# One array tile shape of 64 rows by 64 columns for all stages of a filtered leaky ReLU

## The reference

```python
x = x + sin(W @ coord + b[:, None, None])           # (512, 256, 256), the same for both images
out = x + bias[None, :, None, None]
out = sep_upfirdn(out, up_filter * 2, up=2)          # 256 -> 512 along each axis, 12 taps
out = leaky_relu(out, 0.2) * sqrt(2)                 # on 512 x 512
out = sep_upfirdn(out, down_filter, down=2)          # 512 -> 256 along each axis, 12 taps
```

## Time and profile before

| | |
|---|---|
| runs | 6846.39, 6847.44, 6847.50 us; median 6847.44 us |
| profiled execution | 6846.66 us, its span 6844.9 us |
| TensorE matmul (PE) | 6782.4 us, 99% of the span, 148480 records |
| TensorE weight load (PEld) | 6303.4 us, 92% |
| VectorE (DVE) | 3954.3 us, 58% |
| ScalarE (ACT) | 4084.0 us, 60% |
| GpSimd (POOL) | 1296.0 us, 19% |
| DMA | 82 GB/s over the span |

### The profile page before, as it was taken

One profiled execution on the slowest core, in us unless ns is written; L12 is line 12 of the kernel. 1 busy time (PEld: TensorE's weight loads), 2 busy tenths in 40 slices (PEclk: granted clock), 3 DMA queues, 4 the chain that ended last, 5 costly groups with the idle time before them and its releaser, 6 DMA issues.

```text
span 6844.9 us, 361569 instructions
## 1 busy us (share of the span) xinstructions
PE 6782.4 (99%) x148480; PEld 6303.4 (92%) x148480; DVE 3954.3 (58%) x6218; ACT 4084.0 (60%) x7688; POOL 1296.0 (19%) x1041
## 2 busy tenths in 40 slices
PE   6999999999999999999999999999999999999999
PEld 6999999999999999999999999999999999999998
DVE  6555555555555555555555555555555555555555
ACT  4566566655666665566566656656665665666555
POOL 2111111111111111111111111111111111111111
PEclk9999999999999999999999999999999999999999
DMA  3222222222222222222222222222222222222222
GB/s 116 81 81 81 80 81 81 81 81 81 80 80 81 81 80 81 81 81 81 80 81 81 81 81 81 80 80 81 81 80 81 81 81 80 80 81 81 81 81 74
DMA packets 580065, 558.27 MB, mean 82 GB/s; under 512 B 40400, under 2 KB 574928, under 8 KB 580048
## 3 DMA queue, kind: packets, MB, share of 16 engines
q1 hardware_dynamic: 580048, 558.02, 25.8%
HBM read 278.94 MB, written 278.92 MB: 82 GB/s over the span
## 4 chain that ended last, share of the span: by engine, by line
PE 99%; DVE 1%; issue 0%; DMA 0%; ACT 0%; SPq 0%; DVEq 0%
PE y_ps L450 34%; PE p_ps L434 34%; PE o_ps L434 15%; PE a_ps L450 14%; PE o_ps L460 3%; DVE up_band L377 0%; DVE angle L354 0%; DVE angle L352 0%; DVE phase L344 0%; ACT trig L258 0%; DVE trig_parts L361 0%; DVE angle L356 0%; DVE turns L348 0%; DVE turns L350 0%; DVE trig_parts L360 0%
## 5 line engine op out<-in xcount | busy, mean ns | idle before, releaser
L392 DVE SCALAR_TENSOR_TENSOR z<-y_ps,leak 128x512 f32<-128x512 f32 x4096 | 2716.1, 684 | 1522.9 <-ACT leak L278 1522.9
L278 ACT ACTIVATE leak<-y_ps 128x512 f32<-128x512 f32 x4096 | 2245.3, 605 | 1024.0 <-PE y_ps L450 1024.0
L450 PE MATMUL y_ps<-up_band,a_sb 64*128 64x138 f32 (+2 forms) x32768 | 2807.5, 288 | 1.6 <-ACT a_sb L271 1.5
L434 PE MATMUL p_ps<-down_band,z 128*64 128x68 f32 (+1 forms) x65536 | 2445.9, 227 | 1.8 <-DVE z L392 1.0
L434 PEld LDWEIGHTS p_ps<-down_band,z 128*64 128x64 f32 x65536 | 2156.2, 137 | 267.3 <-DVE z L392 1.3
L450 PEld LDWEIGHTS y_ps<-up_band,a_sb 64*128 64x128 f32 x32768 | 2228.7, 186 | 148.7 <-issue 1.8
L245 POOL TENSOR_TENSOR x_sum<-x_raw,f_sb 128x512 f32<-128x512 f32 x1024 | 1283.6, 1281 | 5514.0 <-ACT f_sb L264 5504.6
L400 DVE COPY p_rows<-p_ps 128x512 f32<-128x512 f32 x2048 | 1411.0, 689 | 1350.4 <-PE p_ps L434 1277.0
L271 ACT COPY a_sb<-a_ps 128x512 f32<-128x512 f32 x2048 | 1100.3, 589 | 1179.8 <-PE a_ps L450 1179.8
L450 PE MATMUL a_ps<-up_band,x_sum 64*128 64x138 f32 (+2 forms) x16384 | 1297.0, 275 | 26.7 <-POOL x_sum L245 26.6
L434 PE MATMUL o_ps<-down_band,p_rows 128*64 128x68 f32 (+1 forms) x32768 | 1171.0, 224 | 0.7 <-issue 0.7
(11 more groups left out here) (28 smaller groups left out, 40.7 us busy)
## 6 DMA issues: line engine op xcount, KB each, us to landing
x_raw<-in_x_dram SPq DMA_DIRECT2D x1024, 256.0 KB, 2.7
out_dram<-o_out SPq DMA_DIRECT2D x1024, 256.0 KB, 2.1
f_rows<-trig_dram SPq DMA_DIRECT2D x512, 20.0 KB
trig_dram<-trig_parts SPq DMA_DIRECT2D x32, 256.0 KB, 2.5
trig_dram<-ones SPq DMA_DIRECT2D x4, 256.0 KB, 2.3
trig_dram<-bias_wide SPq DMA_DIRECT2D x4, 256.0 KB, 2.5
up_taps<-in_L_conv_up_filter_dram SPq DMA_DIRECT2D x1, 6.0 KB, 2.3
down_taps<-_L_conv_down_filter_dram SPq DMA_DIRECT2D x1, 6.0 KB, 2.4
```

The costliest lines, as they stand in the source:

```text
L278: nc.scalar.mul(leak[i % 2][:, :], y_ps[i][:, :], SLOPE * GAIN).then_inc(leak_done, 1)
L392: nc.vector.scalar_tensor_tensor(z[n][:, i, :], y_ps[i][:, :], GAIN, leak[i % 2][:, :], ALU.mult, ALU.max).then_inc(z_done, 1)
L434: last = nc.tensor.matmul(out_ps[half * HALF:(half + 1) * HALF, lo:hi], data[:, t, col:col + HALF], down_band[:, band:band + hi - lo], sta ...
L450: last = nc.tensor.matmul(outs[o][:, lo:hi], data[row, k, (at + o) * P:(at + o + 1) * P], up_band[row, band:band + hi - lo], start=step == ...
```

## The change

All four filter stages and the Fourier term use four tiles of 64 rows by 64 columns. A down stage is now made like an up stage, in two steps with the row tiles changing banks; each 64-row tile covers 36 or 40 output columns. `p_ps` becomes two banks; `o` is written into the banks of `a`, the Fourier term into the two high banks of `y_ps`. The Fourier term is a product of three float32 rows, kept twice (for both row tiles); the split in high and low parts goes. One of the two copies of `a` moves from ScalarE to VectorE (`copy_a1`), behind z1. Every step begins with `pe.sem_inc(steps_begun, 1)`; in the built program that is an event instruction of TensorE's sequencer, and the waits written ahead of it are carried by it or by sequencer instructions in front of it. TensorE's loop body is one channel.

A slot of image m has 13 steps in this order: Y0 step 0, P0 step 0, Y0 step 1, P0 step 1, Fourier (n = 0 only), A step 0, P1 step 0, A step 1, P1 step 1, Y1 step 0, O step 0, Y1 step 1, O step 1. Y0 and Y1 are the bank pairs of `up_cols` of image m, P0 and P1 the two halves of `down_rows` of image m-1 (over z0 and z1, then z2 and z3), A is `up_rows` of image m+1 and O is `down_cols` of image m-2.

Core of the diff (declarations, the setup of the Fourier rows and the unchanged parts of `slot` are cut):

```diff
-    UP_SPAN = [(0, 262, 6), (250, 512, 0)]
+
+    UP_SPAN = [[(0, 132, 6), (122, 260, 128)], [(250, 388, 0), (378, 512, 128)]]
 
-    DN_SPAN = [(0, 68, 4), (60, 132, 0), (124, 196, 0), (188, 256, 0)]
-
-    PE_CHANNELS = 2
-    assert (C - 2) % PE_CHANNELS == 0
+    DN_SPAN = [[(max(0, 32 * g - 4), min(H, 32 * g + 36), max(0, 32 * g - 4) + 4 - 64 * (g // 2)) for g in (2 * k, 2 * k + 1)]
+               for k in range(UT)]
...
-        p_ps = pb("p_ps", [P, 2, H])
-        o_ps = pb("o_ps", [P, HT, WID])
+        p_ps = [pb(f"p_ps{o}", [P, 2, H]) for o in range(2)]
...
+            def copy_a1(m, n):
+
+                dve.wait_ge(a_made, m + 1)
+                reached(dve, y_made, 4 * m - 4)
+                nc.vector.tensor_copy(a_sb[n][:, 1, :], a_ps[1][:, :]).then_inc(a1_copied, 1)
...
+            def copy_p(m, n):
+
+                dve.wait_ge(p_made, m + 1)
+                reached(dve, o_made, m - 1)
+                for o in range(2):
+                    nc.vector.tensor_copy(p_rows[n][:, 2 * o:2 * o + 2, :], p_ps[o][:, :, :]).then_inc(p_copied, 1)
+
+            def slot(c, n, a_next=True, y=True, p=True):
                 m = 2 * c + n
                 if y:
                     leaky(m, n, 0)
+                    leaky(m, n, 1)
+                if a_next:
+                    copy_a1(m + 1, 1 - n)
                 if p:
-                    copy_p(m - 1, 1 - n, 0)
-                if y:
-                    leaky(m, n, 1)
-                if p:
-                    copy_p(m - 1, 1 - n, 1)
+                    copy_p(m - 1, 1 - n)
                 if y:
                     leaky(m, n, 2)
                     leaky(m, n, 3)
...
+            def step_of(outs, data, band, spans, at, where, ks, step, fresh):
+
+                pe.sem_inc(steps_begun, 1)
+                for k in ks:
                     for rows in range(2):
                         o = rows ^ step
                         row = slice(rows * HALF, (rows + 1) * HALF)
-                        lo = max(0, 256 * k + 128 * rows - 6)
-                        hi = min(UP, 256 * k + 128 * rows + 132)
-                        band = lo + 6 - 256 * k
-                        last = nc.tensor.matmul(outs[o][:, lo:hi], data[row, k, (at + o) * P:(at + o + 1) * P],
-                                                up_band[row, band:band + hi - lo], start=step == 0 and k == 0,
-                                                stop=step == 1 and k == HT - 1, skip_group_check=True)
+                        lo, hi, start = spans[k][rows]
+                        for half in range(2):
+                            col = (at + o) * P + half * HALF
+                            last = nc.tensor.matmul(outs[o][half * HALF:(half + 1) * HALF, lo:hi],
+                                                    data[row, where[k], col:col + HALF],
+                                                    band[row, start:start + hi - lo],
+                                                    start=fresh and step == 0 and k == 0,
+                                                    stop=step == 1 and k == len(spans) - 1, skip_group_check=True)
                 return last
 
             def sines(c):
 
-                pe.wait_ge(f_rows_loaded, 16 * c + 16)
-                reached(pe, o_copied, 2 * c - 4)
+                pe.wait_ge(f_rows_loaded, 32 * c + 32)
+                reached(pe, z_done, 8 * c - 8)
+                pe.sem_inc(steps_begun, 1)
                 for t in range(HT):
-                    last = nc.tensor.matmul(o_ps[:, t, :], f_rows[:, t * P:(t + 1) * P], f_rows[:, H:H + WID],
-                                            start=True, stop=True)
+                    row = slice(t * HALF, (t + 1) * HALF)
+                    for half in range(2):
+                        col = t * P + half * HALF
+                        last = nc.tensor.matmul(y_ps[2 + t][half * HALF:(half + 1) * HALF, 0:WID],
+                                                f_rows[row, col:col + HALF], f_rows[row, H:H + WID],
+                                                start=True, stop=True, skip_group_check=True)
                 last.then_inc(f_made, 1)
 
             def up_rows(m, n, step):
                 if step == 0:
                     pe.wait_ge(x_summed, m + 1)
-                    reached(pe, a_copied, m)
-                    up(x_sum[n], a_ps, 0, 0).then_inc(a_half, 1)
+                    reached(pe, o_copied, m - 3)
+                    reached(pe, a0_copied, m)
+                    reached(pe, a1_copied, m)
+                    step_of(a_ps, x_sum[n], up_band, UP_SPAN, 0, range(HT), range(HT), 0, True).then_inc(a_half, 1)
                 else:
                     pe.wait_ge(a_half, m + 1)
-                    up(x_sum[n], a_ps, 0, 1).then_inc(a_made, 1)
-
-            def up_cols(m, n, pair, step):
+                    step_of(a_ps, x_sum[n], up_band, UP_SPAN, 0, range(HT), range(HT), 1, True).then_inc(a_made, 1)
+
+            def up_cols(m, n, pair, step, f_done=0):
                 outs = y_ps[2 * pair:2 * pair + 2]
                 if step == 0:
                     if pair == 0:
-                        pe.wait_ge(a_copied, m + 1)
+                        pe.wait_ge(a0_copied, m + 1)
+                        pe.wait_ge(a1_copied, m + 1)
+                    else:
+                        pe.wait_ge(f_copied, f_done)
                     reached(pe, z_done, 4 * m + 2 * pair - 2)
-                    up(a_sb[n], outs, 2 * pair, 0).then_inc(y_half, 1)
+                    step_of(outs, a_sb[n], up_band, UP_SPAN, 2 * pair, range(HT), range(HT), 0,
+                            True).then_inc(y_half, 1)
                 else:
                     pe.wait_ge(y_half, 2 * m + pair + 1)
-                    up(a_sb[n], outs, 2 * pair, 1).then_inc(y_made, 2)
-
-            def down_rows(m, n, i):
-                if i == 0:
-                    pe.wait_ge(z_done, 4 * m + 4)
-                reached(pe, p_copied, 2 * m + i)
-                for j in range(2):
-                    last = down(z[n], p_ps[:, j, :], (2 * i + j) * P, j == 0)
-                last.then_inc(p_made, 1)
-
-            def down_cols(m, n, f_done):
-                pe.wait_ge(p_copied, 2 * m + 2)
-                reached(pe, o_copied, m)
-                pe.wait_ge(f_copied, f_done)
-                for t in range(HT):
-                    last = down(p_rows[n], o_ps[:, t, :], t * P, t == 0)
-                last.then_inc(o_made, 1)
+                    step_of(outs, a_sb[n], up_band, UP_SPAN, 2 * pair, range(HT), range(HT), 1,
+                            True).then_inc(y_made, 2)
+
+            def down_rows(m, n, late, step):
+
+                if step == 0:
+                    pe.wait_ge(z_done, 4 * m + 2 * late + 2)
+                    if not late:
+                        reached(pe, p_copied, 2 * m)
+                if step or late:
+                    pe.wait_ge(p_part, 3 * m + 2 * late + step)
+                for pair in range(2):
+                    last = step_of([p_ps[o][:, pair, :] for o in range(2)], z[n], down_band, DN_SPAN, 2 * pair,
+                                   range(UT), (2 * late, 2 * late + 1), step, pair == 0)
+                last.then_inc(p_made if late and step else p_part, 1)
+
+            def down_cols(m, n, step):
+                if step == 0:
+                    pe.wait_ge(p_copied, 2 * m + 2)
+                    step_of([a_ps[t][:, 0:WID] for t in range(HT)], p_rows[n], down_band, DN_SPAN, 0,
+                            (0, 2, 1, 3), range(UT), 0, True).then_inc(o_half, 1)
+                else:
+                    pe.wait_ge(o_half, m + 1)
+                    step_of([a_ps[t][:, 0:WID] for t in range(HT)], p_rows[n], down_band, DN_SPAN, 0,
+                            (0, 2, 1, 3), range(UT), 1, True).then_inc(o_made, 1)
 
             def slot(c, n, a_next=True, f_next=True, y=True, p=True, o=True, f_done=None):
                 m = 2 * c + n
                 if y:
                     up_cols(m, n, 0, 0)
+                if p:
+                    down_rows(m - 1, 1 - n, 0, 0)
+                if y:
+                    up_cols(m, n, 0, 1)
+                if p:
+                    down_rows(m - 1, 1 - n, 0, 1)
+                if f_next and n == 0:
+                    sines(c + 1)
                 if a_next:
                     up_rows(m + 1, 1 - n, 0)
-                if y:
-                    up_cols(m, n, 0, 1)
-                if f_next and n == 0:
-                    sines(c + 1)
                 if p:
-                    down_rows(m - 1, 1 - n, 0)
-                if y:
-                    up_cols(m, n, 1, 0)
+                    down_rows(m - 1, 1 - n, 1, 0)
                 if a_next:
                     up_rows(m + 1, 1 - n, 1)
+                if p:
+                    down_rows(m - 1, 1 - n, 1, 1)
+                if y:
+                    up_cols(m, n, 1, 0, c + 2 if f_done is None else f_done)
+                if o:
+
```

(22 more changed lines are left out.)

114 lines of the change are left out of this document (42 added, 72 removed).

## The result

The changed kernel takes 6996.95 us (median of 4 runs, 6993.4 to 7001.07) beside 6846.91 us: a ratio of 1.0219, 95% interval 1.0202 to 1.0237. It is **slower by 150 us**, where 6650 us and "faster" were forecast.

What follows compares the result with a forecast made beforehand. TensorE, busy 99%, was taken as the bound; with the change a channel lasts 12.85 us instead of 13.23, so 6846.7 - 195 (512 channels) - 2 (setup) = 6650 us, range 6430 to 6880 us.

Steps and rivals of the forecast that it cites:

- the new ring through the copy of `a`: O's first step waits for both copies of `a`, whose banks it shares; round trips of 6.04 and 6.81 us.
- the changes of shape: Switching between the up and down filters' array shapes on TensorE costs 0.70 us an image, which would go.
- Rival four: Weights do not bound a TensorE pass, so a down step is 0.29 us: about 6240 us; chance 0.04.
- Rival one: TensorE's run ahead is kept per tile, sixteen instructions for four tiles, hiding more of the gaps: 6510 us; chance 0.22.
- the turn: At TensorE's loop turn, sequencer instructions outlast the queued matmuls and leave a gap of 0.55 us.
- Rival three: Four tiles do not run side by side; loads wait for matmuls on the same rows: about 8650 us; chance 0.06.
- Rival two: Events keep TensorE's weights from being loaded ahead, so the first load behind each lies open: 7100 us; chance 0.10.
- the sum of the ring: Terms from one O step to the next, over both slots, make a channel of 12.85 us.
- The copy's handoff: From the end of `a` on TensorE to the start of VectorE's copy, in slot n = 0: 0.22 us.
- the margin: The forecast saving per channel: 0.38 us, from 13.23 to 12.85 us.
- Slot n = 0: Slot with the loop turn and Fourier; `a` itself, later than z1, decides when its copy starts: 6.81 us.
- Slot n = 1: Slot without Fourier; path runs through ScalarE's leak, z0, z1, then VectorE's copy of `a`: 6.04 us.

Runs made afterwards that it cites:

- 2: Changed kernel with both copies of `a` on ScalarE and none on VectorE: 7366.37 us, ratio 1.076.
- 3: Changed kernel without TensorE's doubled waits, `a` one p step earlier, and VectorE copying `a` ahead of z1: 6486.28 us, ratio 0.9474.
- 4: Changed kernel without TensorE's doubled waits, `a` one p step earlier, VectorE in its old order (z0, z1, `a`): 6587.39 us, ratio 0.9619.
- 6: Changed kernel with 32 instead of 36 to 40 columns in every down filter pass: 6997.8 us, ratio 1.0221.
- 5: Changed kernel with a second sequencer event ahead of every second step, 12 more a channel: 7352.26 us, ratio 1.0741.
- 10: Changed kernel with one channel less written out ahead of TensorE's loop, which starts at channel 2: 7077.47 us, ratio 1.0336.
- 9: Changed kernel with two channels instead of one in TensorE's loop body: 13052.21 us, ratio 1.9068.
- 1: Changed kernel with TensorE's doubled waits dropped (those an earlier wait already covers): 6830.67 us, ratio 0.9976.
- 11: Changed kernel with one channel less written out ahead of TensorE's loop and 32 events (2 KB) put there: 6989.28 us, ratio 1.0209.

## Why the prediction was wrong

**What held.** The mechanism did in the main: the new ring through the copy of `a` paces both slots (2 to 4), the changes of shape cost nothing (the chain), and columns don't pace a down step (6). Rival four falls with the down step itself (0.46 us for its 0.29), and 6 shows that columns don't set it. Rival one falls with the turn, which shows 0.61 us (0.41 and 0.67 - 0.47) and not 0.39. Rival three falls with the down step: eight passes of four tiles in 0.46 us are 0.058 us each, less than a load (0.055 for 64 columns, the prediction's estimate) and its stream (0.034) one after the other. The Trainium skill's rule that weight loads overlap matmuls only in another row group (TensorE: Matmul & The Clock Gate, "Part 3: Packing small matmuls") doesn't hold for these tiles either, and its 60 cycles a matmul (TensorEngine Tiling, "Instruction Overhead") aren't charged to the engine as a whole: 32 matmuls in 0.46 us are 14 ns each. Rival two came to the right side of no change, with 7100 us, yet by luck: no load lies open behind every event, they show where two or more stand together (5).

**The step that failed is the sum of the ring.** The copy's handoff was nearly twice its term (0.39 us for 0.22), nearly all other terms were a little too small, and the margin was 0.38 us of 12.85. By term, measured against forecast (a pair is an up step and a down step):

- Slot n = 0, 7.20 for 6.81. A pair of steps takes 0.93 us (0.47 and 0.46 in the chain), not 0.46 + 0.44: five pairs, +0.15; whether the event in each step has a part in that was not told apart. The turn +0.06 (0.61 for 0.55). Fourier with the gap ahead +0.07 (0.55 for 0.48). The copy of `a` starts on VectorE at 3006.91; the forecast's own terms with these corrections put it at 3006.74, so the handoff is 0.39 for 0.22: +0.17. The 0.22 was read behind a down step of the kernel before; behind an up step, as `a` is one, its rows gave 0.30 (to ScalarE). Back from its end (3007.60) to O 0.31 for 0.37: -0.06.
- Slot n = 1, 6.25 for 6.04. Three pairs +0.09; the gap ahead of Y0 +0.05 (0.57 - 0.47 = 0.10); to ScalarE +0.06; leak to z 0.63 for 0.73, -0.10; two z 1.29 for 1.20, +0.09; from z to the copy 0.09 for nothing; back 0.30 for 0.37, -0.07. Timeline of the changed kernel:

```profile
3011.16 1.08 ACT L272 ACTIVATE leak<-y_ps 128x512 f32<-128x512 f32 x2 [0.41 <-PE y_ps L436]
...
3011.79 1.29 DVE L387 SCALAR_TENSOR_TENSOR z<-y_ps,leak 128x512 f32<-128x512 f32 x2 [0.75 <-ACT leak L272]
...
3013.15 0.58 ACT L266 COPY a_sb<-a_ps 128x512 f32<-128x512 f32 x1 [0.90 <-PE a_ps L436]
3013.17 0.69 DVE L380 COPY a_sb<-a_ps 128x512 f32<-128x512 f32 x1
```

ScalarE's copy of `a` starts at the same time, released by TensorE: in this slot too `a` itself came 0.07 us behind z1. By the forecast's own terms it comes 4.77 us behind the start of O (1.34 + 0.05 + 1.80 + 1.36 + 0.22), 0.21 us ahead of z1's end at 4.98, and I did not count that path for this slot. Measured it is 5.26 us: 0.13 us ahead of `a` (0.60 for 0.47), which I had put at nothing here, five slower pairs (0.15), the gap ahead of Y0 (0.05) and the longer handoff (0.17). So in this slot the path named, through z0 and z1, wasn't the one that ended last, by a hair; with TensorE's order changed it is (4).

Together 0.60 us a channel, 307 us; with the 34 us of start and end, which no term had, 6650 + 307 + 34 = 6991 us, beside 6993.4 of the profiled execution. The range failed because it moved one cost at a time (the pass, or the instruction) on a difference of two nearly equal sums, in which eight of the ten terms erred to the same side. (Its chances for "slower" add up to 0.19, not 0.18.)

**The start and the end.** I counted the added instructions on TensorE nowhere but in its passes. Twice the matmuls are twice the code: ahead of the loop and behind it, it is read once, as it is first run, and TensorE outran the loading (`q8` 23 packets for 14 before; one channel less ahead of the loop saved 9.6 us, 10). Of the 2 us forecast for the setup 0.5 came: the first Fourier copy starts at 50.22 us, before at 50.72. The Trainium skill's Runtime: NRT & Kernel Launch, "Instruction fetch mechanics", says that code streams in 16 KB blocks, mostly hidden, and that TensorE's store holds 128 KB. The blocks' size and the store agree with 9 (two channels' code doesn't stay, one's does); "mostly hidden" does not agree, for matmuls of 14 ns with a load each: 34 us more than before were open here, with what the lower clock cost behind the stalls.

## What to carry to other kernels

When two tiles come to share a bank, write down the ring that closes through it and ask how much independent work stands between the handover and the next writer: here one pair of steps (0.93 us) faced 1.4 us of copy and handoffs, and one step more, with the copy ahead of z1 and the doubled waits gone, turned 2.2% slower into 5.3% faster. Ahead of steps of many short matmuls, waits that are implied already are no longer free: dropping them brought 0.33 us a channel (1), and twelve more events cost 0.69 us (5). How far TensorE runs ahead was only estimated. And when a forecast is a small difference of two sums, vary the terms together.

## What the hardware showed that I had not expected

- Code that is run for the first time by a fast TensorE costs time (some 24 us more than before in the first channels, 10 us in the last), and a loop body past a limit between one and two channels of this code nearly doubles the time (9).
- 2 KB of events in front of a loop, which do nothing, took 0.18 us off each of its turns (10 and 11); at four of five places tried the stall is absent.
- With four tiles a pass of a down step is 0.058 us whatever its 32 to 40 columns; it holds four matmuls and four loads, 7.2 ns each at mean. Whether loads or instructions set it was not told apart.
